# First two key/value products in plain float32 from the loaded blocks, a third warming product, new orders of the steps

## The reference

```python
x = x + L0_xattn(layernorm(x), ctx, ctx, Wq, Wk, Wv, Wo)      # 32 query heads of 16, 8 key/value heads
x = x + L0_ffn(layernorm(x))                                  # x @ W.T + bias, plus low-rank terms for some blocks
x = x + L1_xattn(layernorm(x), ctx, ctx, ...)                 # 16 heads of 32, softmax over batch*heads (axis 0)
x = x + L1_ffn(layernorm(x))                                  # x @ W_base.T + b, plus Fourier-transformed low-rank update

# L0_xattn
k = (key @ Wk);  v = (value @ Wv)
out = softmax((q @ k.T) * scale) @ v
```

## Time and profile before

| | us |
|---|---|
| median of 3 runs | 301.17 |
| the profiled execution | 301.0 |
| its span in the profile | 299.2 |
| TensorE busy | 290.9 |
| VectorE busy | 236.8 |
| ScalarE busy | 163.3 |
| GpSimd busy | 148.0 |

### The profile page before, as it was taken

The page is one execution under the profiler, slowest core; times in us unless marked ns, Lnnn a source line. Parts: engine busy times, 40 slices in busy tenths (PEclk is TensorE's granted clock), DMA queues, the critical chain, the costliest instruction groups (busy, mean ns, idle before and its releaser), DMA issues.

```text
span 299.2 us, 6237 instructions
## 1 busy us (share of the span) xinstructions
PE 290.9 (97%) x2150; PEld 231.5 (77%) x2150; DVE 236.8 (79%) x376; ACT 163.3 (55%) x278; POOL 148.0 (49%) x193
## 2 busy tenths in 40 slices
...
GB/s 221 232 276 194 196 137 300 86 2 248 56 57 94 257 41 107 95 35 2 167 10 53 65 131 68 115 133 134 80 117 111 172 45 99 2 0 38 72 70 105
DMA packets 32136, 33.10 MB, mean 111 GB/s; under 512 B 3608, under 2 KB 21272, under 8 KB 32106
## 3 DMA queue, kind: packets, MB, share of 16 engines
...
...
## 4 chain that ended last, share of the span: by engine, by line
PE 80%; POOL 7%; issue 3%; DMA 3%; DVE 3%; SPq 3%; ACT 1%; POOLq 0%; DVEq 0%; ACTq 0%
PE ps L466 17%; PE ps L468 16%; PE ps L467 16%; PE ps L708 5%; PE ps L630 4%; PE ps L697 4%; PE ps L788 4%; PE ps L675 4%; PE ps L716 3%; PE ps L800 2%; SPq L594 2%; POOL P L1425 2%; DMA ident<-in_eye 1%; POOL ctxT_l L1375 1%; POOL slot_l L1371 1%
## 5 line engine op out<-in xcount | busy, mean ns | idle before, releaser
L1170 DVE TENSOR_REDUCE mx<-ps 128x8 f32<-128x1024 f32 x32 | 38.2, 1217 | 4.2 <-PE ps L675 4.1
L466 PE MATMUL ps<-xT_h,slot_h 128*128 128x256 f32 x128 | 36.9, 288 | 0.1
L968 ACT ACTIVATE PT<-ps 128x1024 f32<-128x1024 f32 x32 | 31.8, 1019 | 8.4 <-PE ps L697 8.3
L468 PE MATMUL ps<-xT_h,slot_l 128*128 128x256 f32 x128 | 35.8, 280 | 0.0
L467 PE MATMUL ps<-xT_l,slot_h 128*128 128x256 f32 x128 | 35.8, 280 | 0.0
L1382 POOL TENSOR_SCALAR var_eps<-moments 128x1 f32<-128x1 f32 x32 | 8.0, 251 | 53.1 <-DVE moments L1133 52.5
L1371 POOL TENSOR_TENSOR slot_l<-stg,slot_h 128x512 fp32r<-128x512 f32 x19 | 25.3, 1337 | 15.8 <-ACT slot_h L896 15.8
L1412 POOL TENSOR_TENSOR zpart<-P 128x512 f32<-128x512 f32 x16 | 20.6, 1289 | 15.1 <-ACT P L1035 13.9
L1187 DVE TENSOR_TENSOR X<-ps,X 128x512 f32<-128x512 f32 x24 | 16.4, 683 | 12.5 <-PE ps L468 8.4
L466 PEld LDWEIGHTS ps<-xT_h,slot_h 128*128 128x128 f32 x128 | 24.2, 189 | 2.3 <-issue 0.7
L1403 POOL TENSOR_TENSOR KM_h<-K_h,own 128x512 fp32r<-128x512 f32 x8 | 8.6, 1075 | 32.2 <-DVE K_l L1157 26.0
...
## 6 DMA issues: line engine op xcount, KB each, us to landing
...
```

Source lines behind the costliest of these rows:

```text
L466: eng.matmul(dst, left[0], right[0], start=start, stop=False)
L468: return eng.matmul(dst, left[1], right[0], start=False, stop=stop)
L968: act.activation(PT[:, g2, :], wide(step).rearrange("p k n -> p (k n)"), ACT.Exp, scale=SCALE0).then_inc(act_freed, 1)
L1170: dve.tensor_reduce(mx[:, b % 2, :].rearrange("p (x r) -> p r x", r=REP)[:, r, :], wide(step).rearrange("p k (g t) -> p (k g) t", g=4), AX ...
```

## The change

1. Of the two `V0` steps in `PLAIN` (blocks 0 and 1) each becomes plain float32 straight from the loaded context block and the loaded `wkv` chunks: for each of the four contraction chunks four matmuls, each with 32 columns of the context block as stationary operand, which write 32 PSUM partitions each, 256 columns wide. Their four splits (`CT.0.0`, `CT.0.1` on ScalarE, `CL.0.0`, `CL.0.1` on VectorE) go. `wkv` is still split, for blocks 2 to 7.
2. The two `wkv` chunks and the context blocks 2 and 3 (`AHEAD`) land in `PT`, not in `stg` and `ctx_in`; so the first four `wq0` chunks find empty slots in `stg`. The first exponential waits until the two plain steps and the splits of `wkv` are done, the second until blocks 2 and 3 are split.
3. `WARM` is 3.
4. All five lists are laid out anew. TensorE's steps are the same 286 in another order and with other banks, SyncE's 117 and GpSimd's 104 too; ScalarE and VectorE lose two each.

The diff, cut to its core (of the lists the lines on which something below rests):

```diff
-WARM = 2
...
 SP_TEXT = """
-LX.0 LX.1 LC.0.0 LW.wkv.0 LI LW.wkv.1 LC.0.1 LW.wq0.0 LW.wq0.1 LW.wq0.2 LW.wq0.3 LX.3 LX.2 LC.0.2 LX.4 LC.0.3
-LW.wo.2 LX.5 LW.wo.0 LW.la.0 KL.0 QL.0 LO DM.0 LW.wo.1 LX.6 LC.0.5 LX.7 LC.0.4 QL.1 DM.1 KL.1 LW.wo.3 LS QL.2 DM.2
...
-LW.wbase.1 LC.2.2 LC.2.3 LC.2.1 LB LC.2.0 OUT.6 OUT.7 OUT.4 OUT.5 OUT.2 OUT.3 OUT.0 OH.1.1 OH.1.0
+LX.0 LX.1 LC.0.0 LW.wkv.0 LI LW.wkv.1 LC.0.1 LW.wq0.0 LW.wq0.1 LW.wq0.2 LX.2 LW.wq0.3 LC.0.2 LX.3 LX.5 LC.0.3 LX.4
+LC.0.5 KL.0 LC.0.4 LW.wo.2 LO LW.wo.3 QL.0 DM.0 LX.6 LW.wo.1 LS QL.1 LW.wo.0 DM.1 KL.1 LW.la.0 LX.7 LC.0.7 QL.2 DM.2
...
+LW.wbase.3 LC.2.3 LC.2.0 LC.2.1 OUT.6 OUT.7 OUT.4 OUT.5 OUT.2 OUT.3 OH.1.1 OUT.0 OH.1.0
...
 PE_TEXT = """
-XT.0.1:5 XT.0.0:3 V0.0:7 V0.1:5 Q0.0.0:1 K0.0:4 Q0.0.1:7 MX.0.1:0 MX.0.0:2 V0.2:5 MX.0.3:6 MX.0.2:0 XT.0.2:4 V0.3:2
-XT.0.3:0 K0.1:1 MT.0:3 MX.1.3:6 MX.1.2:4 MX.1.0:2 Q0.1.0:0 ST.0.3:4 ST.0.2:6 Q0.1.1:1 ST.0.0:2 MX.1.1:6 XT.0.5:0
...
-OX1.6:1 V1.0:2 PV1.4:0 PV1.5:1 OX1.4:2 OX1.7:3 V1.1:0 XT.3.6:1 PV1.2:3 PV1.3:2 OX1.5:0 F1.6:3 OX1.3:1 XT.3.7:2
-OX1.2:0 XT.3.4:3 PV1.0:1 PV1.1:2 F1.7:0 OX1.0:2 XT.3.5:1 OX1.1:3 F1.4:0 XT.3.2:3 F1.5:2 XT.3.3:0 F1.2:3 XT.3.0:1
-F1.3:0 XT.3.1:2 F1.0:1 FH.1.1:3 FH.1.0:0
+XT.0.1:4 XT.0.0:7 V0.0:0 V0.1:1 Q0.0.0:5 K0.0:0 Q0.0.1:6 MX.0.1:4 MX.0.0:0 V0.2:3 MX.0.3:6 MX.0.2:4 XT.0.3:2 V0.3:3
+XT.0.2:0 K0.1:1 MT.0:3 MX.1.0:6 MX.1.1:4 MX.1.2:2 Q0.1.0:0 ST.0.3:4 ST.0.2:2 ST.0.1:6 Q0.1.1:1 ST.0.0:4 MX.1.3:6
...
+OX1.6:1 V1.0:3 PV1.4:0 PV1.5:2 OX1.7:0 V1.1:1 XT.3.6:3 OX1.4:2 PV1.3:1 PV1.2:0 OX1.5:2 F1.6:3 OX1.3:1 OX1.2:2
+XT.3.7:0 XT.3.4:3 PV1.1:1 PV1.0:2 F1.7:0 OX1.1:2 OX1.0:1 XT.3.5:3 F1.4:0 XT.3.2:3 F1.5:1 XT.3.3:2 F1.2:0 XT.3.0:3
+F1.3:2 XT.3.1:1 F1.0:0 FH.1.1:1 FH.1.0:3
...
-SET.8 LNn.0.0 W.wkv.0 CT.0.0 W.wkv.1 XT.0.1 CT.0.1 W.wq0.0 XT.0.0 W.wq0.1 W.wq0.2 V0.0 W.wq0.3 V0.1 K0.0 Q0.0.0
-CT.0.2 CT.0.3 Q0.0.1 LNn.0.2 V0.2 LNn.0.3 XT.0.2 V0.3 XT.0.3 MT.0 W.wo.2 LNn.0.4 K0.1 Q0.1.0 ST.0.3 W.la.0 W.wo.1
...
+SET.8 W.wkv.0 LNn.0.0 W.wkv.1 XT.0.1 XT.0.0 W.wq0.0 W.wq0.1 W.wq0.2 V0.0 W.wq0.3 V0.1 CT.0.2 K0.0 Q0.0.0 CT.0.3
+Q0.0.1 LNn.0.2 LNn.0.3 V0.2 XT.0.3 V0.3 XT.0.2 MT.0 W.wo.2 LNn.0.4 K0.1 CT.0.5 W.wo.3 Q0.1.0 ST.0.3 ST.0.2 ST.0.1
...
-SET.6 LNs.0.0 LNs.0.1 C0 LNn.0.1 L.wkv.0 CL.0.0 XT.0.1 CL.0.1 XT.0.0 L.wq0.1 LNs.0.3 LNs.0.2 K0.0 LNs.0.4 Q0.0.0
...
-V1.7 FF.1 NM.12 NM.15 NM.14 NM.8 NM.9 NM.11 OX1.6 NM.10 LNs.3.6 NM.7 NM.6 OX1.7 NM.5 LNs.3.7 FF.0 OX1.4 LNs.3.4
-XT.3.6 NM.2 NM.0 OX1.5 F1.6 OX1.3 XT.3.7 OX1.2 LNs.3.5 LNs.3.2 LNs.3.3 LNn.3.5 XT.3.4 F1.7 OX1.0 OX1.1 XT.3.5
-LNn.3.2 LNs.3.1 F1.4 LNs.3.0 XT.3.2 LNn.3.0 F1.5 LNn.3.1 XT.3.3 XT.3.0 F1.2 F1.3 XT.3.1 F1.0 FH.1.1 FH.1.0
+SET.6 LNs.0.0 LNs.0.1 LNn.0.1 L.wkv.0 XT.0.1 XT.0.0 C0 L.wq0.1 LNs.0.2 LNs.0.3 K0.0 CL.0.2 Q0.0.0 LNs.0.4 MX.0.1
+Q0.0.1 MX.0.0 MX.0.3 MX.0.2 XT.0.3 XT.0.2 MX.1.1 MX.1.2 MX.1.0 K0.1 LNs.0.5 LNn.0.5 Q0.1.0 CL.0.5 MX.1.3 XT.0.5
...
+NM.10 NM.9 NM.11 NM.8 OX1.6 FF.0 LNs.3.6 NM.5 NM.7 OX1.7 LNs.3.7 NM.6 XT.3.6 OX1.4 LNs.3.4 NM.0 OX1.5 NM.2 F1.6
+OX1.3 OX1.2 XT.3.7 LNs.3.5 LNs.3.2 XT.3.4 LNs.3.3 LNn.3.5 F1.7 OX1.1 OX1.0 LNn.3.2 XT.3.5 LNs.3.0 F1.4 LNn.3.0
+XT.3.2 LNs.3.1 F1.5 XT.3.3 F1.2 LNn.3.1 XT.3.0 F1.3 XT.3.1 F1.0 FH.1.1 FH.1.0
...
-L.wbase.1 NM.4 LNs.3.6 L.wbase.3 XB.6 LNs.3.7 NM.3 LNs.3.4 NM.1 LNs.3.5 XB.7 LNs.3.3 XB.4 LNs.3.2 XB.5 LNs.3.0
-LNs.3.1 XB.2 XB.3 XB.0 XB.1
+SET.1 SET.2 SET.0 LNs.0.0 LNs.0.1 L.wkv.1 L.wq0.0 L.wq0.2 L.wq0.3 KM.0 LNs.0.2 LNs.0.3 CL.0.3 KM.1 LNs.0.4 L.wo.2
...
+L.wbase.2 CL.2.1 LNs.3.6 NM.3 XB.6 L.wbase.1 LNs.3.7 LNs.3.4 NM.1 XB.7 XB.4 LNs.3.2 LNs.3.5 LNs.3.3 XB.5 LNs.3.0
+XB.2 LNs.3.1 XB.3 XB.0 XB.1
...
-CHUNKS = [s[1:] for s in SP_ORDER if s[0] == "LW"]
+CHUNKS = [s[1:] for s in SP_ORDER if s[0] == "LW" and s[1] != "wkv"]
...
+PLAIN = (("V0", 0), ("V0", 1))
+AHEAD = (2, 3)
+CTX_IN = {step: n for n, step in enumerate(s for s in CTX if s[1] or s[2] not in AHEAD)}
...
+        def ctx_source(eng, use, b):
+
+            if ("LC", use, b) not in CTX_IN:
+                eng.wait_ge(ahead_loaded[AHEAD.index(b)], 16)
+                return early(2 + AHEAD.index(b))
+            n = CTX_IN[("LC", use, b)]
+            eng.wait_ge(ctx_loaded[n % 2], 16 * (n // 2 + 1))
+            return ctx_in[:, n % 2, :]
...
+        def early(k):
+
+            return PT[:, k // 2, k % 2 * D:(k % 2 + 1) * D]
...
+            if key[0] == "wkv":
+
+                return early(key[1])
             return stg[:, CHUNK[key] % NSTG, :]
...
+                    use, b = step[1:]
+                    if step not in CTX_IN:
+                        k = AHEAD.index(b)
+                        sp.dma_start(early(2 + k), ctx[b]).then_inc(ahead_loaded[k], 16)
+                        continue
+                    n = CTX_IN[step]
                     if n >= 2:
 
-                        ctx_split(sp, *at(CTX, n - 2)[1:])
-                    sp.dma_start(ctx_in[:, n % 2, :], ctx[step[2]]).then_inc(ctx_loaded[n % 2], 16)
+                        old = at(CTX_IN, n - 2)[1:]
+                        if ("V0", old[1]) in PLAIN and old[0] == 0:
+                            filled(sp, ("V0", old[1]))
+                        else:
+                            ctx_split(sp, *old)
+                    sp.dma_start(ctx_in[:, n % 2, :], ctx[b]).then_inc(ctx_loaded[n % 2], 16)
...
+                    if step in PLAIN:
+
+                        src = ctx_source(pe, 0, b)
+                        for c in range(C):
+                            stage_loaded(pe, ("wkv", c // 2))
+                            for j in range(4):
+                                last = pe.matmul(dst[32 * j:32 * j + 32, 0:2 * P],
+                                                 src[:, c * P + 32 * j:c * P + 32 * j + 32],
+                                                 stage(("wkv", c // 2))[:, c % 2 * 2 * P:(c % 2 + 1) * 2 * P],
+                                                 start=(c == 0), stop=(c == C - 1))
+                        last.then_inc(psum_full, 1)
+                        continue
...
+                    elif g2 == 0:
+                        all_filled(act, PLAIN)
+                        for c in range(2):
+                            chunk_split(act, ("wkv", c))
+                    elif g2 == 1:
+                        for early_b in AHEAD:
+                            ctx_split(act, 0, early_b)
...
```

More of the change, by code:

```diff
@@ L91 @@
+W.wbase.1 V1.4 V1.3 V1.2 PV1.6 CT.2.1 PV1.7 PV1.4 V1.0 FP.0 PV1.5 LNn.3.6 V1.1 XT.3.6 LNn.3.7 PV1.2 PV1.3 LNn.3.4
+XT.3.7 PV1.1 XT.3.4 PV1.0 LNn.3.3 XT.3.5 XT.3.2 XT.3.3 XT.3.0 XT.3.1
 """
 DVE_TEXT = """
[L94 to L96 removed]
```

131 lines of the change are left out of this document (68 added, 63 removed).

## The result

The changed kernel takes 297.36 us in the median of four executions (297.09 to 297.65) against 301.06 us for the kernel before beside it; the ratio is 0.989 with a 95% interval of 0.987 to 0.991. Run again on another chip it took 298.10 us (297.15 to 299.73) against 300.67, ratio 0.992 (0.989 to 0.995).

The account below looks back on a forecast made before the run. TensorE, busy 290.9 of 299.2 us, was taken as the bound. Start 0.6, form changes 0.5 and last layer 0.6 gave 1.7 us off 301.0, 299.3; with runs' median 0.2 above that execution, forecast 299.4, range 298.0 to 301.7.

Parts of the forecast that it names:

- The start: Start of the kernel: earlier transposes and Q0.0.0 at 12.45 bring first maxima to 18.5; 0.6 us gained, between 0 and 1.0.
- the key mask: GpSimd at the start: the mask, 17.42 to 18.46 before, would end near 17.6 and not be late.
- the bound of 1.0: Upper end of the predicted gain at the start, in us, if nothing waits for wq0.
- The rival in which it falls all the same: Start: TensorE's clock drops to half from 8.8 to 12.2 us, maxima at 20.1, total 300.9 us; chance 0.17.
- the third product: Third warming product before the first transposes: costs nothing, shrinks TensorE's 2.28 us idle to 0.3 to 1.1, clock doesn't fall.
- The form changes: TensorE's list: neighbours of different form fall from 160 to 154, 0.09 us each; 0.5 us gained, bounds 0 and 0.5.
- gain in layer 0: Rival, 20 to 140 us: several sums of waits change by a quarter, giving 297.8 to 298.8 us; chance 0.18.
- The last layer: GpSimd's new order normalises block 2 earlier, removing TensorE's idle time before its transposes at 280.64; 0.6 us gained.
- The rival of the store of block 6: Last layer: XB.4 waits for this store, delaying roots of blocks 2 and 5; 301.8 us; slower case's chance 0.10.
- SyncE and the exponentials' new waits: Loads issued without waits, wo.2 later; first two exponentials wait for splits ending before 23 us; cost nothing.
- The sum: 0.6 (start) + 0.5 (forms) + 0.6 (last layer) = 1.7 us off 301.0, giving 299.3, forecast 299.4.
- the 0.2 added: Median of the runs lies 0.2 us above the profiled execution, so 299.3 became a forecast of 299.4.

Follow-up runs that it names:

- the separate matmuls: Kernel before plus unread matmuls behind its last TensorE step, each kind alone, then in turns; full and two halves 0.86 us a round where the sum is 0.50.

## Why the prediction was right or wrong

- **The start, +0.6 us predicted, +1.06 in the profile, +0.7 in the second profile of the same kernel.** Its steps stand: the clock holds at 1.00 through the transposes and value steps; a plain value step takes 1.83 us (predicted 1.85); Q0.0.0 goes behind GpSimd's low half; nobody waits for the key mask (GpSimd, 16.26 to 17.68). What was too late is the point where it begins: the split of the weights starts at 6.33 where the earlier trace rows had 6.74, and Q0.0.0 at 12.01 for 12.45. In nine profiles with this start the weights' split starts between 5.91 and 7.12 and the first maxima between 17.99 and 18.75, with a median of 18.40, 0.7 us ahead of 19.12. So the 0.6 was about right, and some 0.3 us of the first profile's lead belong to that execution. The profile lies just beyond the bound of 1.0.
- **The clock.** The rival in which it falls all the same did not come about. The rows show the high level through eight transposes after 0.36 us of idle time. For the rival the prediction cited the Trainium skill, TensorE: Matmul & The Clock Gate, Part 4, which says that transposes do not count as busy in the same way; these eight did not bring the clock down. But what the prediction did not see is that the fall is not in every execution of the kernel before: of its 103 executions timed beside the experiments, 44 had a mean clock of 0.994 or less and took 300.93 us in the median, the others 300.37. One profile showed one outcome, and the sum took it for the rule. A mean of 1.00 is no proof of the high level either: in the run with the separate matmuls, which starts as the kernel before, it is 1.00, the warming records end before the clock has risen, the transposes start 0.21 us apart, and the first maxima come at 21.34. So the third product guards against two things, a fall and a clock that has not risen; the prediction knew the first alone.
- **The form changes, +0.5 us predicted, +1.4 to 1.5 measured in layer 0.** This is the step that failed: the prediction's 6 x 0.09, in both factors. The price of 0.09 us was read off one pair of neighbours, a full matmul ahead of column tiles; it holds only what lies ahead of the change, and about as much lies behind it. By the separate matmuls a change costs 0.18 us between full and half height, 0.15 between full and tiles, and in its place in layer 0 0.14 to 0.16. The count mixed tiling with data type, which costs nothing. By tiling alone the whole list falls by six as well, from 97 to 91, but that is eight fewer in layer 0 (70 to 62) and two more from the plain steps, which belong to the start. Eight times 0.14 to 0.18 is 1.1 to 1.4; 0.25 us of less waiting in layer 0, which the term did not have, make up the rest. The upper bound of this term, 0.5, was its own value; a price taken from one pair needed a second one, and 49 changes between full and half height stood in the trace of layer 0.
- **The rival "gain in layer 0"** gave 297.8 to 298.8 by shorter waits. Its time holds the second result (298.10) and is the nearest to the first, its mechanism was in the main another: summed over the view of waits, from the first maxima to the end of layer 0, the weight loads waited 13.5 us for other engines and transfers before and 16.5 in the changed kernel. What fell is the time in which they waited for nothing that the profile shows, 46 times and 14.2 us before, 32 times and 9.5 us after.
- **The last layer, +0.6 predicted, +0.8 measured.** Right in its mechanism, idle time ahead of block 2 taken away by GpSimd's new order, though the old order takes it away too in some executions; the runs showed that the long normalised block was a collision with the addition of block 5. The rival of the store of block 6 did not come: its successor waited 0.45 us at 269.75.
- **SyncE and the exponentials' new waits** cost nothing that shows: TensorE's waits in the changed kernel are 1.9 us for its first operands, 0.6 for normalised blocks and 0.2 for a low half of the queries.
- **The sum** added terms that were right in sign. With the price and count of the experiments it would have been 0.6 + 1.4 + 0.8 = 2.8 us off 301.0, with the 0.2 added as in the prediction 298.4; the changed kernel took 297.36 us and 298.10 us in its two comparisons. No version tried here is faster than the changed kernel.
